# Cross-attention row maximum over partitions: GpSimd all-reduce in place of two groups of TensorE transposes, with exponentials two beats later

## The chip, the cores and the metric

One NeuronCore of a Trainium2 chip runs the whole program. The metric is the device time of one execution in microseconds (us). Engines: TensorE (PE in the profile, PEld for its weight loads), VectorE (DVE), ScalarE (ACT), GpSimd (POOL), and SyncE (SP), whose queue issues the DMAs.

## The reference

One layer of a perceiver on `x` (8 x 128 x 512, f32) with a context of 8 x 2048 x 512:

```python
x = x + xattn(layernorm(x), ctx, ctx)      # 16 heads of 32, 128 queries, 2048 keys
x = x + diff_attn(layernorm(x))            # two causal softmaxes a head, their difference
x = x + ffn(layernorm(x))                  # 8 experts with softmax gates
# within xattn:
scores = einsum('bhqd,bhkd->bhqk', q, k) / sqrt(32)
attn = softmax(scores, axis=-1)
ctx = einsum('bhqk,bhkd->bhqd', attn, v)
```

The change is in xattn alone, in the maximum that softmax subtracts.

## The kernel before

The program is a row of stages, each a block of its own on all engines: queries and weights, cross attention, output projection, the projections of self attention, differential attention, experts. Cross attention (`cross_attention`, L318 to L762) is the longest.

**Slots.** The work of cross attention is cut into 32 slots (8 batches times G = 4 groups of HG = 4 heads). A slot has four chunks of 512 keys. The order of work is written out by hand in beats, eight to a slot. `steps(beat, first, every, count)` says which item of a kind falls on a beat, and each engine runs the same loop over all beats, doing what the beat asks of it in the order of its own code.

**What a beat holds on PE** (L622 to L640). Every beat projects one unit of keys or values, twelve matmuls (L560, L567, through `product`, L43 to L45). Even beats also transpose context (L552), multiply one chunk of exponentials by the values (`outputs`, L601) and make one chunk of scores (`column_scores`, L587). Once a slot `denominators` (L611) multiplies the summed exponentials by ones. Beats that come up below, modulo 8: score chunks 0 to 3 of a slot on beats 4, 6, 0 and 2 (20, 22, 24, 26 for slot 0). All score chunks share one set of PSUM banks, `psS`, so PE waits for `s_moved` before the next.

**The maximum.** Scores lie with keys over the partitions and (head, query) along the free dimension, so the maximum over keys is one over chunks and partitions. DVE folds each chunk into `mx` (L759 copies the first piece of a slot, L762 folds the other fifteen); there is one `mx`. Then PE transposes `mx` (`turn("M", ...)`, beat 27), DVE reduces it to `top` (L726), ACT spreads that (L700), PE transposes back (`turn("B", ...)`, beat 28) and ACT copies the result to `mb` (L692). So every partition has one maximum for a head and a block of 128 queries.

**After the maximum.** ACT moves each score chunk from PSUM to one of BUFS = 6 buffers `s` (L713, on the beat after its scores). DVE subtracts `mb` from it (L733), ACT takes the exponential (L705), PE reads it for the outputs (L601) and POOL adds it up in `acc`: one add for chunk 0 (L512), two for each other (L517). POOL's chunk 0 waits for the denominators of the slot before (`od_full`). ACT may fill a buffer again when PE and POOL are done with its old content (`pv_done`, `sum_done`, L709 to L712).

**Banks.** Context transposes, projections and both kinds of turn share three PSUM banks `work` in a ring (`RING`, L379 to L391).

**Elsewhere** POOL broadcasts a row over partitions once in each of three later stages (`partition_broadcast`, L827, L1168, L1504), each time followed by `tensor_tensor` operations (L831, L1184, L1508).

## Time and profile before

| what | value |
|---|---|
| time, median of 3 runs | 1859.81 us (1859.74 to 1862.59) |
| the profiled execution's own time | 1860.6 us |
| its span in the trace | 1858.2 us |
| mean granted TensorE clock over the span | 0.955 |
| PE busy, share of the span | 1716.2 us, 92% |
| DVE busy | 1224.5 us, 66% |
| ACT busy | 962.7 us, 52% |
| POOL busy | 776.3 us, 42% |

The profiled execution's time is its span and 2.4 us around it. Times in rows count from the start of the span. Busy shares are means over stages with different limits; a sum for a change in cross attention has to be read from that stage.

### The profile page before, as it was taken

Reading aid. Unit: us, or ns where it says so; the run is one execution under the profiler, and the core shown is the slowest. Engines: PE = TensorE matmul, PEld = TensorE weight load, DVE = VectorE, ACT = ScalarE, POOL = GpSimd, SP = SyncE. Lnnn points to the kernel's source line nnn. Section 1 sums busy time; section 2 is a strip of 40 time slices with the busy share of each in tenths; the row PEclk is TensorE's granted clock in tenths of the full one; section 3 lists DMA queues with packets and bytes.
Section 4 is the critical chain, followed back from the end, with each engine's and each line's share of the span. In section 5 each row is a group of like instructions: output and inputs, shape, how many; then the busy total and the mean of one; then the engine's idle time right before and its main releaser. Section 6 shows DMA issues by size and latency. Waiting matters only on the chain. (4 is left out here: it accounts for less than half of the span.)

```text
span 1858.2 us, 36962 instructions
## 1 busy us (share of the span) xinstructions
PE 1716.2 (92%) x15305; PEld 1377.4 (74%) x15320; DVE 1224.5 (66%) x1631; ACT 962.7 (52%) x1470; POOL 776.3 (42%) x343
## 2 busy tenths in 40 slices
PE   6899999999999999999999997538999689879999
PEld 5688888888888888888888875437887466658886
DVE  5126887887887787787787788957332677753223
ACT  2236666666666666666666665533220677731000
POOL 0002555555555555555555555662000466622210
PEclk9999999999999999999999998658999899989999
DMA  4211111111111111110110102103650533201101
GB/s 162 69 46 38 38 29 40 38 28 40 38 30 38 38 34 34 38 40 28 38 41 27 38 7 71 44 29 131 201 179 14 159 92 90 68 24 46 45 23 45
DMA packets 104189, 104.94 MB, mean 56 GB/s; under 512 B 7263, under 2 KB 72799, under 8 KB 104044
## 3 DMA queue, kind: packets, MB, share of 16 engines
q1 hardware_dynamic: 104044, 102.83, 18.2%
q8 instruction: 113, 1.85, 0.4%
q14 instruction: 32, 0.26, 0.0%
HBM read 79.74 MB, written 23.07 MB: 55 GB/s over the span
## 5 line engine op out<-in xcount | busy, mean ns | idle before, releaser
L517 POOL TENSOR_TENSOR b_acc<-b_acc,b_s 128x1024 f32<-128x1024 f32 x192 | 525.7, 2738 | 294.6 <-ACT b_s L705 282.3
L733 DVE TENSOR_TENSOR b_s<-b_s,b_mb 128x2048 f32<-128x2048 f32 x128 | 372.5, 2912 | 15.7 <-ACT b_mb L692 15.7
L762 DVE TENSOR_TENSOR b_mx<-b_psS,b_mx 128x512 f32<-128x512 f32 x480 | 331.1, 690 | 44.2 <-PE b_psS L587 31.1
L705 ACT ACTIVATE b_s<-b_s 128x2048 f32<-128x2048 f32 x128 | 245.1, 1915 | 89.3 <-DVE b_s L733 89.3
L713 ACT ACTIVATE b_s<-b_psS 128x2048 f32<-128x2048 f32 x128 | 241.1, 1884 | 50.8 <-DVE b_mx L762 50.4
L43 PE MATMUL b_work<-cT,wkT 128*128 128x512 f32 x512 | 211.0, 412 | 0.0
L43 PE MATMUL b_work<-wvT,cT 128*128 128x512 f32 x512 | 209.4, 409 | 0.0
L512 POOL TENSOR_TENSOR b_acc<-b_s 128x1024 f32<-128x1024 f32 x32 | 80.8, 2525 | 290.8 <-PE b_psO L611 179.8
L44 PE MATMUL b_work<-cT,wkT 128*128 128x512 f32 x512 | 201.0, 393 | 0.0
L45 PE MATMUL b_work<-cT,wkT 128*128 128x512 f32 x512 | 200.7, 392 | 0.0
L45 PE MATMUL b_work<-wvT,cT 128*128 128x512 f32 x512 | 200.2, 391 | 0.0
L44 PE MATMUL b_work<-wvT,cT 128*128 128x512 f32 x512 | 200.0, 391 | 0.0
L587 PE MATMUL b_psS<-b_q,b_kT 32*128 32x128 f32 x4096 | 157.4, 292 | 15.1 <-ACT b_s L713 15.1
L664 ACT ACTIVATE b_kT<-b_work,b_bk 128x512 f32<-128x512 f32 x128 | 88.1, 688 | 157.4 <-PE b_work L45 155.0
L587 PEld LDWEIGHTS b_psS<-b_q,b_kT 32*128 32x128 f32 x4096 | 132.3, 194 | 41.6 <-issue 41.4
L601 PE MATMUL b_psO<-b_s,v_sb 128*32 128x128 f32 x4096 | 147.3, 289 | 15.6 <-ACT b_s L705 12.9
L601 PEld LDWEIGHTS b_psO<-b_s,v_sb 128*32 128x32 f32 x4096 | 111.9, 115 | 44.3 <-issue 43.7
L752 DVE TENSOR_TENSOR cT<-b_work,cT 128x512 fp32r<-128x512 f32 x128 | 87.3, 683 | 84.4 <-ACT cT L697 84.4
L1648 DVE SCALAR_TENSOR_TENSOR x<-f_ps,f_gate,x 128x512 f32<-128x512 f32 x64 | 47.9, 750 | 119.8 <-PE f_ps L45 119.3
L43 PEld LDWEIGHTS b_work<-cT,wkT 128*128 128x128 f32 x512 | 96.6, 189 | 30.1 <-issue 5.6
L43 PEld LDWEIGHTS b_work<-wvT,cT 128*128 128x128 f32 x512 | 96.1, 188 | 24.4
L45 PEld LDWEIGHTS b_work<-cT,wkT 128*128 128x128 f32 x512 | 96.7, 189 | 21.5
(221 smaller groups left out, 3036.7 us busy)
## 6 DMA issues: line engine op xcount, KB each, us to landing
cin<-in_ctx SPq DMA_DIRECT2D x64, 512.0 KB, 3.7
q_scratch<-d_st SPq DMA_DIRECT2D x32, 256.0 KB, 2.5
k_scratch<-d_st SPq DMA_DIRECT2D x32, 256.0 KB, 2.5
e_q<-q_scratch SPq DMA_DIRECT2D x16, 512.0 KB, 3.5
k_sb<-k_scratch SPq DMA_DIRECT2D x64, 128.0 KB, 3.6
experts_sb<-in_L_ffn_expert_w SPq DMA_DIRECT2D x8, 1024.0 KB, 5.2
x_sb<-in_x SPq DMA_DIRECT2D x2, 1024.0 KB, 7.1
q_scratch<-a_q SPq DMA_DIRECT2D x4, 512.0 KB, 3.2
```

The source lines that it names most:

```text
L43: nc.tensor.matmul(out, lhs[0], rhs[0], start=first, stop=False)
L44: nc.tensor.matmul(out, lhs[0], rhs[1], start=False, stop=False)
L45: return nc.tensor.matmul(out, lhs[1], rhs[0], start=False, stop=last)
L517: nc.gpsimd.tensor_tensor(acc[:, :, :], acc[:, :, :], s[:, buf, 2 * i:2 * i + 2, :], ALU.add).then_inc(sum_done, 1)
L587: last = nc.tensor.matmul(psS[:, j, t * P:(t + 1) * P], kT[h, at + t * P:at + (t + 1) * P], q[h, m % 3, :], start=True, stop=True)
L601: last = nc.tensor.matmul(psO[j * HD:(j + 1) * HD, 0:P], v[:, at + j * HD:at + (j + 1) * HD], s[:, n % BUFS, i, j * P:(j + 1) * P], start= ...
L664: nc.scalar.activation(kT[:, at:at + 512], work[i % BANKS][:, :], ACT.Identity, bias=bk[:, u:u + 1]).then_inc(k_done, 1)
L705: nc.scalar.activation(part, part, ACT.Exp, scale=SCALE).then_inc(exp_done, 1)
L713: nc.scalar.activation(s[:, n % BUFS, :, :].rearrange("p t (j q) -> p t j q", j=HG), psS[:, :, :].rearrange("p j (t q) -> p t j q", t=CHUN ...
L733: nc.vector.tensor_tensor(s[:, n % BUFS, :, :], s[:, n % BUFS, :, :], mb[:, :].rearrange("p (o n) -> p o n", o=1).broadcast_to([P, CHUNK, ...
L752: nc.vector.tensor_tensor(context_place(cT[1], p, n), two(work[RING["T", p, n] % BANKS]), f32(context_place(cT[0], p, n)), ALU.subtract).t ...
L762: nc.vector.tensor_tensor(mx[:, :, :], part, mx[:, :, :], ALU.max).then_inc(mx_done, 1)
```

## The change

The new kernel has POOL reduce `mx` over the partitions with one `partition_all_reduce` for each slot, [128 x 512] to [128 x 512], straight to `mb`. Both turns on PE, the reduction on DVE and two ACT copies for each slot are removed, and their bank uses with them. `mb` has two buffers in place of one. The maximum stands in POOL's order on beat 27, behind the sums of beat 26 and ahead of those of beat 28. Subtractions, exponentials, outputs, sums and denominators come two beats later, and `s` has seven buffers. DVE's first piece of a slot's `mx` (L759) now waits for `mb_done`, the end of the all-reduce of the slot before.

```diff
--- before.py
+++ after.py
@@ -328,8 +328,8 @@
         SLOTS = B * G
         SLOT = 8
         CHUNK = 4
-        BUFS = 6
-        FIRST, LAST = -SLOT, (SLOTS + 4) * SLOT + 3
+        BUFS = 7
+        FIRST, LAST = -SLOT, (SLOTS + 4) * SLOT + 5
         ADDS = 2 * CHUNK - 1
         MAXIMA = CHUNK * CHUNK
 
@@ -353,27 +353,21 @@
         def move_step(beat):
             return score_step(beat - 1)
 
-        def turned_slot(beat):
-            return steps(beat, 27, SLOT, SLOTS)
-
-        def spread_slot(beat):
-            return steps(beat, 28, SLOT, SLOTS)
-
         def exp_step(beat):
-            return steps(beat, 30, 2, SLOTS * CHUNK)
+            return steps(beat, 32, 2, SLOTS * CHUNK)
 
         def value_step(beat):
 
-            early, late = steps(beat, 32, 2, SLOTS * CHUNK), steps(beat, 33, 2, SLOTS * CHUNK)
+            early, late = steps(beat, 34, 2, SLOTS * CHUNK), steps(beat, 35, 2, SLOTS * CHUNK)
             if early is not None and early % CHUNK:
                 return early
             return late if late is not None and late % CHUNK == 0 else None
 
         def sum_slot(beat):
-            return steps(beat, 40, SLOT, SLOTS)
+            return steps(beat, 42, SLOT, SLOTS)
 
         def normal_slot(beat):
-            return steps(beat, 40, SLOT, SLOTS)
+            return steps(beat, 42, SLOT, SLOTS)
 
 
         BANKS = 3
@@ -384,10 +378,6 @@
             if (x0 := projected(beat)) is not None:
                 p0, u0 = x0
                 RING["KV"[u0 // CHUNK], p0, u0 % CHUNK] = len(RING)
-            if (s0 := turned_slot(beat)) is not None:
-                RING["M", s0, 0] = len(RING)
-            if (s0 := spread_slot(beat)) is not None:
-                RING["B", s0, 0] = len(RING)
         UNITS = list(RING)
 
         def key_place(b, g, c):
@@ -409,9 +399,7 @@
         q = sb("b_q", [P, 3, P])
         s = sb("b_s", [P, BUFS, CHUNK, HG * P])
         mx = sb("b_mx", [P, HG, P])
-        top = sb("b_top", [P, 2, HG])
-        spread = sb("b_spread", [P, HG, P])
-        mb = sb("b_mb", [P, HG * P])
+        mb = sb("b_mb", [P, 2, HG * P])
         acc = sb("b_acc", [P, 2, HG * P])
         rD = sb("b_rD", [P, P])
         oq = sb("b_oq", [P, P])
@@ -430,8 +418,6 @@
         v_done = sem("b_v_done")
         mx_done = sem("b_mx_done")
         s_moved = sem("b_s_moved")
-        top_done = sem("b_top_done")
-        spread_done = sem("b_spread_done")
         mb_done = sem("b_mb_done")
         s_full = sem("b_s_full")
         sub_done = sem("b_sub_done")
@@ -501,7 +487,8 @@
         @block.gpsimd
         def _(pool):
             nc.gpsimd.memset(ones[:, :], 1.0).then_inc(const, 1)
-            for n in range(SLOTS * CHUNK):
+
+            def sums(n):
                 m, c = divmod(n, CHUNK)
                 buf = n % BUFS
                 pool.wait_ge(exp_done, n + 1)
@@ -517,6 +504,21 @@
                         nc.gpsimd.tensor_tensor(acc[:, :, :], acc[:, :, :], s[:, buf, 2 * i:2 * i + 2, :],
                                                 ALU.add).then_inc(sum_done, 1)
 
+            def maximum(m):
+
+                pool.wait_ge(mx_done, (m + 1) * MAXIMA)
+
+                reached(pool, sub_done, (m - 1) * CHUNK)
+                nc.gpsimd.partition_all_reduce(mb[:, m % 2, :], mx[:, :, :].rearrange("p j q -> p (j q)"),
+                                               P, RMAX).then_inc(mb_done, 1)
+
+            for beat in range(FIRST, LAST):
+                if (n := exp_step(beat)) is not None:
+                    sums(n)
+                n = score_step(beat - 1)
+                if n is not None and n % CHUNK == CHUNK - 1:
+                    maximum(n // CHUNK)
+
         def sums_of(n):
 
             m, c = divmod(n, CHUNK)
@@ -534,12 +536,8 @@
                         pe.wait_ge(split_done, m * CHUNK + n + 1)
                     elif kind == "K":
                         pe.wait_ge(k_done, m * CHUNK + n + 1)
-                    elif kind == "V":
+                    else:
                         pe.wait_ge(v_done, m * CHUNK + n + 1)
-                    elif kind == "M":
-                        pe.wait_ge(top_done, m + 1)
-                    else:
-                        pe.wait_ge(mb_done, m + 1)
                 return work[i % BANKS]
 
             def transposes(p, n):
@@ -612,13 +610,6 @@
                                                 acc[:, i, j * P:(j + 1) * P], start=i == 0, stop=i == 1)
                 last.then_inc(od_full, 1)
 
-            def turn(kind, m, src, ready, count):
-                bank = bank_of((kind, m, 0))
-                pe.wait_ge(ready, count)
-                for j in range(HG):
-                    last = nc.tensor.transpose(bank[:, j * P:(j + 1) * P], src[:, j, :], ident[:, :])
-                last.then_inc(work_full, 1)
-
             for beat in range(FIRST, LAST):
                 if (x0 := transposed(beat)) is not None:
                     transposes(*x0)
@@ -634,10 +625,6 @@
                         keys(p, u)
                     else:
                         values(p, u - CHUNK)
-                if (m := turned_slot(beat)) is not None:
-                    turn("M", m, mx, mx_done, (m + 1) * MAXIMA)
-                if (m := spread_slot(beat)) is not None:
-                    turn("B", m, spread, spread_done, m + 1)
 
         def context_place(a, p, n):
 
@@ -684,21 +671,11 @@
                                 out = rows[:, :, at[0]:at[0] + P]
                             nc.scalar.activation(out, work[i % BANKS][:, :].rearrange("p (g r) -> p g r", g=G),
                                                  ACT.Copy).then_inc(v_done, 1)
-                if (m := spread_slot(beat - 1)) is not None:
-                    i = RING["B", m, 0]
-                    act.wait_ge(work_full, i + 1)
-
-                    reached(act, sub_done, m * CHUNK)
-                    nc.scalar.activation(mb[:, :], work[i % BANKS][:, :], ACT.Copy).then_inc(mb_done, 1)
                 if (x0 := transposed(beat)) is not None:
                     p, n = x0
                     i = RING["T", p, n]
                     act.wait_ge(work_full, i + 1)
                     nc.scalar.activation(context_place(cT[0], p, n), two(work[i % BANKS]), ACT.Copy).then_inc(hi_done, 1)
-                if (m := spread_slot(beat)) is not None:
-                    act.wait_ge(top_done, m + 1)
-                    nc.scalar.activation(spread[:, :, :], top[:, m % 2, :].rearrange("p (j o) -> p j o", o=1)
-                                         .broadcast_to([P, HG, P]), ACT.Copy).then_inc(spread_done, 1)
                 if (n := exp_step(beat)) is not None:
                     act.wait_ge(sub_done, n + 1)
                     part = s[:, n % BUFS, :, :].rearrange("p t n -> p (t n)")
@@ -718,13 +695,6 @@
         def _(dve):
             dve.wait_ge(bias_in, 32)
             for beat in range(FIRST, LAST):
-                if (m := spread_slot(beat)) is not None:
-                    i = RING["M", m, 0]
-                    dve.wait_ge(work_full, i + 1)
-
-                    reached(dve, spread_done, m - 1)
-                    nc.vector.tensor_reduce(top[:, m % 2, :], work[i % BANKS][:, :].rearrange("p (j k) -> p j k", j=HG),
-                                            AX.X, ALU.max).then_inc(top_done, 1)
                 if (n := exp_step(beat)) is not None:
                     m, c = divmod(n, CHUNK)
                     dve.wait_ge(s_moved, n + 1)
@@ -732,7 +702,7 @@
                         dve.wait_ge(mb_done, m + 1)
                     nc.vector.tensor_tensor(
                         s[:, n % BUFS, :, :], s[:, n % BUFS, :, :],
-                        mb[:, :].rearrange("p (o n) -> p o n", o=1).broadcast_to([P, CHUNK, HG * P]),
+                        mb[:, m % 2, :].rearrange("p (o n) -> p o n", o=1).broadcast_to([P, CHUNK, HG * P]),
                         ALU.subtract).then_inc(sub_done, 1)
                 if (m := normal_slot(beat)) is not None:
                     g = m % G
@@ -756,6 +726,9 @@
                     for t in range(CHUNK):
                         part = psS[:, :, t * P:(t + 1) * P]
                         if n % CHUNK == 0 and t == 0:
+                            if n:
+
+                                dve.wait_ge(mb_done, n // CHUNK)
                             nc.vector.tensor_copy(mx[:, :, :], part).then_inc(mx_done, 1)
                         else:
                             dve.wait_ge(mx_done, n * CHUNK + t)
```

## Rows read from the trace of the kernel before

**Rows 1.** Windows of the cross attention: busy time and instructions of each engine, clock, DMA.
```profile
200.00:1130.00 930.00, 930.00 (x10559) 751.97 (x10558) 737.99 (x751) 613.08 (x589) 505.81 (x189) 1.00 0.12 34
1130.00:1248.00 118.00, 58.36 (x950) 46.23 (x948) 94.35 (x74) 53.62 (x34) 80.06 (x28) 0.60 0.15 47
```

**Rows 2.** Timeline, PE, one slot: start, duration, instructions merged.
```profile
608.83 1.17 PE L587 MATMUL b_psS<-b_q,b_kT 32*128 32x128 f32 x32
...
616.04 0.64 PE L611 MATMUL b_psO<-b_acc,b_ones 128*32 128x128 f32 x16
616.62 1.17 PE L587 MATMUL b_psS<-b_q,b_kT 32*128 32x128 f32 x32
...
625.06 1.08 PE L601 MATMUL b_psO<-b_s,v_sb 128*32 128x128 f32 x32
626.07 1.17 PE L587 MATMUL b_psS<-b_q,b_kT 32*128 32x128 f32 x32
...
632.76 0.60 PE L619 MATMUL b_work<-ident,b_mx 128*128 128x128 f32 x4
633.20 0.60 PE L552 MATMUL b_work<-ident,cin 128*128 128x128 f32 x4
```

**Rows 3.** Timeline, DVE: the first piece of a slot's maximum.
```profile
153.26 0.68 DVE L759 COPY b_mx<-b_psS 128x512 f32<-128x512 f32 x1
...
1119.76 0.69 DVE L759 COPY b_mx<-b_psS 128x512 f32<-128x512 f32 x1
...
1182.40 0.68 DVE L759 COPY b_mx<-b_psS 128x512 f32<-128x512 f32 x1
```

**Rows 4.** Timeline, POOL, around partition_broadcasts: idle time before in brackets.
```profile
1253.80 1.04 POOL L827 PARTITION_BROADCAST c_bo<-c_bo_row  x1 [9.23 <-issue]
1264.12 10.04 POOL L831 TENSOR_TENSOR x<-x,c_bo 128x512 f32<-128x512 f32 x8 [9.27 <-issue]
...
1452.86 0.31 POOL L1168 PARTITION_BROADCAST e_coef<-e_coef_row  x1 [6.65 <-issue]
1463.02 2.03 POOL L1184 TENSOR_TENSOR e_sm<-e_sm,e_cf 128x512 f32<-128x512 f32 x2 [9.84 <-issue]
...
1662.99 4.57 POOL L1508 TENSOR_TENSOR f_ws<-experts_sb,f_ws 128x2048 fp32r<-128x2048 f32 x1 [6.92 <-issue]
```

**Rows 5.** Groups of instructions, POOL: count, busy, mean ns of one, idle before.
```profile
L1184 POOL TENSOR_TENSOR e_sm<-e_sm,e_cf 128x512 f32<-128x512 f32 x64 | 73.5, 1150 | 61.2 <-DVE e_cf L1378 50.7 <-issue 9.8
L1190 POOL TENSOR_TENSOR e_root<-e_ms,e_expo 128x16 f32<-128x16 f32 x8 | 23.3, 2907 | 7.1 <-DVE e_ms L1406 7.0
```

**Rows 6.** Timeline, DVE and PE, where PE waits for the move of scores.
```profile
1136.13 2.85 DVE L762 TENSOR_TENSOR b_mx<-b_psS,b_mx 128x512 f32<-128x512 f32 x4
...
1141.04 2.09 PE L587 MATMUL b_psS<-b_q,b_kT 32*128 32x128 f32 x32 [4.05 <-ACT b_s L713]
...
1171.33 1.76 PE L587 MATMUL b_psS<-b_q,b_kT 32*128 32x128 f32 x32 [2.23 <-ACT b_s L713]
```

**Rows 7.** Timeline, POOL, chunks 0 and 1 of a slot's sums.
```profile
616.87 2.39 POOL L512 TENSOR_TENSOR b_acc<-b_s 128x1024 f32<-128x1024 f32 x1 [6.34 <-PE b_psO L611]
619.40 4.88 POOL L517 TENSOR_TENSOR b_acc<-b_acc,b_s 128x1024 f32<-128x1024 f32 x2
```

**Rows 8.** Instructions of L733, DVE, and of L517, POOL: least, median and longest ns.
```profile
L733 DVE TENSOR_TENSOR b_s<-b_s,b_mb x128: 2277/2794/4448, 157.3 to 1228.1; 128x2048 f32<-128x2048 f32 x128
...
L517 POOL TENSOR_TENSOR b_acc<-b_acc,b_s x192: 2337/2407/4353, 170.2 to 1242.2; 128x1024 f32<-128x1024 f32 x192
```

**Rows 9.** Timeline, PE, a stretch behind idle time early in cross attention.
```profile
60.14 1.09 PE L552 MATMUL b_work<-ident,cin 128*128 128x128 f32 x4 [2.37 <-DMA cin<-in_ctx]
...
65.72 0.45 PE L45 MATMUL b_work<-cT,wkT 128*128 128x512 f32 x1
```

**Rows 10.** Timeline, DVE: last piece of slot 0's maximum; and PE: the last denominators.
```profile
145.74 2.86 DVE L762 TENSOR_TENSOR b_mx<-b_psS,b_mx 128x512 f32<-128x512 f32 x4
...
1244.62 1.08 PE L611 MATMUL b_psO<-b_acc,b_ones 128*32 128x128 f32 x16 [8.04 <-POOL b_acc L517]
```

## The prediction

> **What bounds the kernel now.** I began with the windows of the cross attention. From 200 to 1130 us PE is busy all 930 us at a granted clock of 1.00 (the 2.4 GHz level), DVE for 738, ACT for 613, POOL for 506 [rows 1]: this stretch is as long as PE's list. Behind it the projections have run out, and a slot is paced by the chain between PE, DVE and ACT: PE is busy 58 of 118 us, the clock falls to 0.60 [rows 1]. The first piece of a slot's maximum shows the rhythm: 28 slots from 153.26 to 1119.76, 34.52 us each, then two more in 62.64 us, and after the last of them 63.3 us until the last denominators end at 1245.70 [rows 3, 10]. The stages behind are not touched.
>
> Next I read POOL's timeline wherever it does what it does nowhere in cross attention, that is, around partition_broadcast. Each such instruction, and the first tensor_tensor behind it, stands behind idle time that no wait explains ("issue"): 9.23 and 6.65 us ahead of the broadcasts, 9.27, 9.84 and 6.92 ahead of the tensor_tensors [rows 4]. POOL changes kind of code there. In the new kernel it would do so twice in every slot.
>
> **What it removes.** The turn of `mx` puts the next unit of PE from 632.76 to 633.20: 0.44 us; the turn of `spread` has the same four transposes, so 0.88 us a slot, and PE's list becomes 33.64 us. The reduction on DVE and the two copies on ACT lay on engines with time to spare and count nothing. The ring of banks loses two uses, which can only help.
>
> **What it adds.** One all-reduce for each slot. The trace has none, so I bound its duration R. Below: no less than the broadcast of a 512-column row, 1.04 us [rows 4]. Above, if it went column by column like the power operation (2907 ns for 16 columns [rows 5]), 512 columns would take 93 us. In between: 128 partitions are seven halvings, and one two-input operation on 512 columns costs 1.15 us [rows 5], so 8.05 us. I take 8.05, because the halvings are what a maximum needs at least when it is done on whole vectors. Two passes for each halving would make 16.1.
>
> **The changes of code.** All-reduce and tensor_tensor alternate in POOL's order: chunk 0 and 1 of the sums, all-reduce, chunk 2 and 3. I assume that the all-reduce belongs with the broadcast. Ahead of it I take 6.65 us (the smaller, since the other may hold a DMA's landing), behind it the mean of the three, 8.68 [rows 4]. Of the same load the Trainium skill (GPSIMD Engine Reference, 2.1 Instruction dispatch) says that the first call to freshly loaded code pays about 6 us, 5.95 measured, with no instruction to be seen. The trace agrees for the way in (6.65); with 5.95 the sum below would be some 22 us less.
>
> **The new wait.** DVE's first piece of slot m+1 waits until the all-reduce of slot m ends, since there is one `mx`. Behind that wait stand, in DVE's own order, the rest of the chunk's maxima; ACT waits for those to move the scores, and PE for the move before its next score group. So a loop goes around once a slot:
> - From the end of the all-reduce through four maxima and a move to PE's scores of chunk 1: 1136.13 to 1141.04, 4.91 us [rows 6].
> - From there to the scores of chunk 3 PE must do its list: 608.83 to 626.07, 17.24, less one group of outputs (625.06 to 626.07, 1.01) that now falls outside: 16.23 [rows 2]. The two turns lie outside this part, so their removal doesn't shorten the loop.
> - The denominators come directly ahead of that group, and POOL's chunk 0 starts 0.25 us behind the group's start (616.62, 616.87) [rows 2, 7]. Chunks 0 and 1 take until 624.28, 7.41 us [rows 7]. L733 takes 2277 ns at least and 4448 at most, L517 2337 and 4353 [rows 8]: they exclude each other. One subtraction falls into these adds now that no reduction holds DVE up: 2.17. Together 9.83. The last chunk's maxima are done earlier than that (1.17 and 2.86 us) and hold nothing up.
> - Change of code 6.65, all-reduce 8.05.
>
> That is 21.14 + 9.83 + 14.70 = 45.67 us. PE has 33.64 to do and stands idle 12 us in one piece, ahead of chunk 1's scores. Behind 4.05 us of idle time that group took 2.09 us in place of 1.17 [rows 2, 6], the level of 1.2 GHz; and after such an interruption PE worked slowly from 60.14 to 65.72, which costs half of 5.58: 2.79 [rows 9]. So 48.46 us a slot.
>
> The other change of code, 8.68 us, comes behind the all-reduce, beside PE's list: chunks 2 and 3 (2 x 4.88) are then done 18.4 us after it, the denominators at about 21. With seven buffers ACT's move of chunk 1 needs chunk 2's sum, 13.6 us after the all-reduce against some 9 that it would like; PE would feel 2 to 4 us of this, but it runs beside the slow stretch just counted, so I add nothing. The later beats cost nothing in themselves: every item shifts alike. SP's queue holds the same loads and stores, those of `o` two beats later.
>
> **The sum.**
> - Slot 0: its maxima end at 148.60 [rows 10], the code is already loaded, so the next first piece comes at 156.65, not 153.26: +3.4.
> - 28 slots x 48.46 = 1356.9 against 966.5 [rows 3]: +390.4.
> - Two slots of the tail: scores follow each other every 7.57 us (1141.04 to 1171.33 is four [rows 6]), so 4.91 + 15.15 + 9.83 + 14.70 = 44.59 each, against 62.64 for both: +26.5.
> - The end: 44.59 for the last maximum, 8.68 to change code, chunks 2 and 3 at 9.76, denominators 1.33, four chunks 17.17, denominators 1.08: 82.6 against 63.3: +19.3.
>
> Together +439.6 us on the profiled execution's 1860.6: 2300 us. The median of the three runs is 0.8 us lower, which is nothing here. Every microsecond of R counts 32 times: 2300 + 32 x (R - 8.05).
>
> **Rivals.**
> 1. Column by column. For it speaks the power operation, 182 ns a column; against it, that a plain operation takes 2.2. With 93 us the time would be about 5020. The Trainium skill (GPSIMD Engine Reference, 3.2 Cross-partition) gives 247,699 ns for a reduction along the partition axis of 128 x 2048, a quarter of which, 62 us, is an estimate for 512 columns and would make 4026. No row here shows it. Chance 0.12.
> 2. No change of code between all-reduce and adds, with R near the broadcast's: the faster side. The loop is then 30.97 + R; it meets PE's list of 33.64 at R = 2.7 and the old slot of 34.52 at R = 3.55, and that is the point that decides. At R = 1.04: 28 x 0.88 = 24.6 us in the slots, 0.8 in the tail and 3.0 at the end, 1832 us. Against it stand the five gaps of rows 4. Chance 0.05. The same without a change of code but with R = 8.05: 39.0 and 2.8 for the clock, in all about 2085; chance 0.04, inside the range.
> 3. The move does not hide the latency but no engine waits long: if POOL fetches the other code while still adding, the gaps vanish under work. The gap behind L827 lies between two POOL instructions with nothing to cover it, so the trace can't exclude this; here the adds run to the last moment as well. It gives the times of rival 2, and its chance is counted there.
>
> **The numbers.** Forecast (code changed twice a slot, R between 1.04 and 16.1): chance 0.79. Low end: R = 1.04 gives 2076, and without the loss of clock (28 x 2.79) 1998. High end: R = 16.1 gives 2558, and if all four subtractions of a slot stand in POOL's way, 3 x 2.17 x 28 = 182 more, 2740. Range 2000 to 2740. A measurement can tell about 0.2%, 3.7 us, from no change. Faster 0.04, same 0.01, slower 0.95.
>
> **What would show it.** In the new profile: two gaps "issue" a slot in POOL's timeline, of 6 to 10 us; the all-reduce at about 8 us; the copy into `mx` idle before it with POOL as the releaser, some 16 us long; PE's L587 waiting for ACT's move about 12 us once a slot, its digits of clock below 9; first pieces 48 us apart. I am wrong if the gaps are absent, if R lies far from 8, or if the first piece does not wait for POOL.

## The result, and the profile after

The new kernel takes 2024.17 us, the median of four runs (2016.55 to 2042.29), beside 1860.92 for the kernel before (1859.74 to 1862.59): a ratio of 1.0891, 95% interval 1.0813 to 1.0968. It is slower by 163 us, where 440 was forecast. The profiled execution took 2019.06 us, its span 2017.3, which is 159.1 more than before. The new kernel's runs differ by 26 us, the old one's by 3; a possible reason is given behind the experiments.

The page of the new kernel, span, engines and the clock in 40 slices:

```profile
span 2017.3 us, 36462 instructions
...
PE 1740.0 (86%) x15064; PEld 1391.7 (69%) x15064; DVE 1201.1 (60%) x1599; ACT 925.2 (46%) x1406; POOL 829.0 (41%) x375
...
PEclk9999999999999989999998999655899989999999
```

No engine became the bound: every share has fallen. PE's own work grew by 24 us although 256 transposes are gone, because part of it ran at a lower clock. The digits hardly show that; a window over the slots does, and the tail behind them (columns: stretch, its length, PE, PEld, DVE, ACT, POOL busy with instructions, clock, DMA share, GB/s):

```profile
200.00:1290.00 1090.00, 979.61 (x10614) 786.15 (x10613) 748.71 (x742) 595.62 (x544) 570.92 (x223) 0.94 0.11 32
1290.00:1400.00 110.00, 40.48 (x688) 32.93 (x688) 67.39 (x54) 39.84 (x21) 66.97 (x25) 0.53 0.08 21
```

Before, PE was busy for all of such a stretch at clock 1.00 [rows 1]. Now it stands for 110 of 1090 us.

**Where the time came from.** Below, "the change in" is the idle time of POOL ahead of an all-reduce that follows adds, "the change back" the one ahead of the adds that follow an all-reduce. DVE's first pieces of a slot's maximum, now L732, and the last denominators on PE, now L609 (timelines: start, duration, idle time before and its releaser):

```profile
153.37 0.68 DVE L732 COPY b_mx<-b_psS 128x512 f32<-128x512 f32 x1
...
1254.31 0.69 DVE L732 COPY b_mx<-b_psS 128x512 f32<-128x512 f32 x1 [5.81 <-POOL b_mb L512]
...
1330.88 0.69 DVE L732 COPY b_mx<-b_psS 128x512 f32<-128x512 f32 x1 [5.67 <-POOL b_mb L512]
```

```profile
1407.39 1.08 PE L609 MATMUL b_psO<-b_acc,b_ones 128*32 128x128 f32 x16 [8.04 <-POOL b_acc L504]
```

Against [rows 3, 10]:

| part | before | after | added | forecast |
|---|---|---|---|---|
| until the first piece of slot 1 | 153.26 | 153.37 | +0.1 | +3.4 |
| 28 slots | 966.5 (34.52 each) | 1100.94 (39.32 each) | +134.4 | +390.4 |
| two slots of the tail | 62.64 | 76.57 | +13.9 | +26.5 |
| from there to the end of the last denominators | 63.3 | 77.6 | +14.3 | +19.3 |

Together +162.8; the stages behind gave back 3.7. So 28 slots hold nearly all of it, and there the forecast was 9.1 us a slot too high.

**One slot.** POOL's timeline from the end of one all-reduce (625.68 + 1.80 = 627.48) to the end of the next:

```profile
625.68 1.80 POOL L512 PARTITION_ALL_REDUCE b_mb<-b_mx  x1 [5.87 <-issue]
634.19 11.71 POOL L504 TENSOR_TENSOR b_acc<-b_acc,b_s 128x1024 f32<-128x1024 f32 x4 [6.71 <-issue]
...
650.25 2.39 POOL L499 TENSOR_TENSOR b_acc<-b_s 128x1024 f32<-128x1024 f32 x1 [4.36 <-PE b_psO L609]
652.79 4.88 POOL L504 TENSOR_TENSOR b_acc<-b_acc,b_s 128x1024 f32<-128x1024 f32 x2
663.56 1.80 POOL L512 PARTITION_ALL_REDUCE b_mb<-b_mx  x1 [5.89 <-issue]
```

DVE's, ACT's and PE's timelines in that slot:

```profile
627.58 0.69 DVE L732 COPY b_mx<-b_psS 128x512 f32<-128x512 f32 x1 [5.02 <-POOL b_mb L512]
...
656.02 3.80 DVE L703 TENSOR_TENSOR b_s<-b_s,b_mb 128x2048 f32<-128x2048 f32 x1
```

```profile
639.15 1.89 ACT L690 ACTIVATE b_s<-b_psS 128x2048 f32<-128x2048 f32 x1 [0.40 <-POOL b_acc L504]
```

```profile
632.50 2.09 PE L585 MATMUL b_psS<-b_q,b_kT 32*128 32x128 f32 x32 [2.62 <-ACT b_s L690]
...
642.22 1.17 PE L585 MATMUL b_psS<-b_q,b_kT 32*128 32x128 f32 x32
...
650.01 1.17 PE L585 MATMUL b_psS<-b_q,b_kT 32*128 32x128 f32 x32
```

The loop of the prediction is there step by step. The all-reduce ends, DVE starts its piece 0.10 us later, PE its scores of chunk 1 after 5.02 us (632.50), behind 2.62 us of idle time and at the lower of the clock's two levels, 1.2 GHz (2.09 us, where the same group takes 1.17 at 2.4 GHz). Chunk 3's scores follow 17.51 us on, chunk 0's sum 0.24 later, the adds of chunks 0 and 1 take 7.42, the change of code 5.89 and the all-reduce 1.80: 37.9 us. The mean spacing of all-reduces from slot 2 to slot 28 (slots counted from 0) is 39.4.

**Where other slots spend more.** Every one of these 26 slots has the same 5.0 us from the all-reduce to chunk 1's scores and nearly the same 15.4 us (13.5 to 13.8, and the 1.8 of the all-reduce) from chunk 3's scores to the end of the next all-reduce. What differs lies between. A row of the waits, 300 to 1200 us (total, times, longest), and one of the longer slots in ACT's and PE's timelines, behind an all-reduce that ended at 704.67:

```profile
ACT b_s L690 <- POOL b_acc L504: 42.1, 17, 4.6
```

```profile
718.71 1.88 ACT L690 ACTIVATE b_s<-b_psS 128x2048 f32<-128x2048 f32 x1 [2.66 <-POOL b_acc L504]
```

```profile
709.70 1.17 PE L585 MATMUL b_psS<-b_q,b_kT 32*128 32x128 f32 x32 [2.62 <-ACT b_s L690]
...
720.73 1.17 PE L585 MATMUL b_psS<-b_q,b_kT 32*128 32x128 f32 x32 [1.14 <-ACT b_s L690]
```

Here the scores of chunk 1 (709.70) stand behind the same 2.62 us of idle time and yet run at the upper level, and ACT's move of chunk 1 waits 2.66 us for chunk 2's sum, the last user of the buffer it wants. That sum stands behind the change back. This is a second loop, through the change back and the buffers of `s`. In 14 of the 26 slots the move waits for it by 2.0 to 4.8 us, and in 11 of those chunk 1's scores ran in 1.17 us. In the other 12 it waits less than 1 us, and in 11 of those chunk 1's scores took 1.5 to 2.1 us. So either the lower clock or the wait for the sum holds up a slot: chunk 2's scores come 10.6 us behind chunk 1's on average in the one kind of slot and 11.1 in the other.

The queue of POOL's instructions (POOLq) shows more of the idle time called "issue". All instructions of L512 and of L504 (counts; for L512 least, median and longest ns):

```profile
L512 POOLq MODIFY_POOL_CONFIG  x64: 1/13/30, 53.5 to 1359.6; - x64
L512 POOL PARTITION_ALL_REDUCE b_mb<-b_mx x32: 1802/1803/1807, 149.1 to 1366.4; - x32
  issue: 184.9, 31
...
L504 POOLq MODIFY_POOL_CONFIG  x62: 98/98/98, 191.6 to 1368.2; - x62
```

POOL's configuration is changed ahead of each all-reduce and again ahead of the adds behind it; 184.9 us in 31 gaps are 5.96 each on the way in. What POOL does in the gap is not seen: the two DMA queues of the kind "instruction" carried no more than before (111 and 33 packets against 113 and 32).

### The profile page after: what moved, and what is told of

Read it like the earlier page. It is cut to its first block and busy times, and to the rows that moved or that the text cites. A ratio compares the mean times of both kernels' runs of the same rounds, so it can differ in the third digit from the quotient of the medians.

```text
span 2017.3 us, 36462 instructions
## 1 busy us (share of the span) xinstructions
PE 1740.0 (86%) x15064; PEld 1391.7 (69%) x15064; DVE 1201.1 (60%) x1599; ACT 925.2 (46%) x1406; POOL 829.0 (41%) x375
## 5 line engine op out<-in xcount | busy, mean ns | idle before, releaser
L504 POOL TENSOR_TENSOR b_acc<-b_acc,b_s 128x1024 f32<-128x1024 f32 x192 | 522.7, 2722 | 246.0 <-issue 191.0
L585 PE MATMUL b_psS<-b_q,b_kT 32*128 32x128 f32 x4096 | 169.7, 308 | 143.0 <-ACT b_s L690 143.0
L585 PEld LDWEIGHTS b_psS<-b_q,b_kT 32*128 32x128 f32 x4096 | 144.3, 208 | 171.8 <-issue 166.6
L43 PE MATMUL b_work<-wvT,cT 128*128 128x512 f32 x512 | 222.6, 435 | 0.0
L43 PE MATMUL b_work<-cT,wkT 128*128 128x512 f32 x512 | 213.5, 417 | 0.0
L44 PE MATMUL b_work<-wvT,cT 128*128 128x512 f32 x512 | 212.0, 414 | 0.0
L45 PE MATMUL b_work<-wvT,cT 128*128 128x512 f32 x512 | 211.0, 412 | 0.0
L44 PE MATMUL b_work<-cT,wkT 128*128 128x512 f32 x512 | 203.7, 398 | 0.0
L45 PE MATMUL b_work<-cT,wkT 128*128 128x512 f32 x512 | 202.9, 396 | 0.0
L512 POOL PARTITION_ALL_REDUCE b_mb<-b_mx x32 | 57.7, 1803 | 280.6 <-issue 184.9
L43 PEld LDWEIGHTS b_work<-wvT,cT 128*128 128x128 f32 x512 | 104.9, 205 | 29.6 <-issue 3.4
L45 PEld LDWEIGHTS b_work<-wvT,cT 128*128 128x128 f32 x512 | 103.9, 203 | 24.4
L43 PEld LDWEIGHTS b_work<-cT,wkT 128*128 128x128 f32 x512 | 98.3, 192 | 30.9 <-ACT b_kT L651 5.6
```

The lines of the kernel that those rows point to most:

```text
L43: nc.tensor.matmul(out, lhs[0], rhs[0], start=first, stop=False)
L44: nc.tensor.matmul(out, lhs[0], rhs[1], start=False, stop=False)
L45: return nc.tensor.matmul(out, lhs[1], rhs[0], start=False, stop=last)
L504: nc.gpsimd.tensor_tensor(acc[:, :, :], acc[:, :, :], s[:, buf, 2 * i:2 * i + 2, :], ALU.add).then_inc(sum_done, 1)
L585: last = nc.tensor.matmul(psS[:, j, t * P:(t + 1) * P], kT[h, at + t * P:at + (t + 1) * P], q[h, m % 3, :], start=True, stop=True)
```

## The experiments

"Slot" is the mean spacing of all-reduces (or of what stands in their place) from slot 2 to slot 28; in the new kernel 39.4 us. The kernel before took 1859 to 1861.5 us beside each.

**1. No change of code.** The all-reduce is replaced by POOL's own kind of operation, `mx - mx`. No maximum is taken.

```diff
-                nc.gpsimd.partition_all_reduce(mb[:, m % 2, :], mx[:, :, :].rearrange("p j q -> p (j q)"),
-                                               P, RMAX).then_inc(mb_done, 1)
+                nc.gpsimd.tensor_tensor(mb[:, m % 2, :], mx[:, :, :].rearrange("p j q -> p (j q)"),
+                                        mx[:, :, :].rearrange("p j q -> p (j q)"), ALU.subtract).then_inc(mb_done, 1)
```

> The changed kernel with a tensor_tensor of POOL (mx minus mx, 512 columns) in the all-reduce's place: the exponentials are then taken without a maximum, and POOL never changes its code inside cross attention; every wait stays. Theory: the 5.9 us ahead of the all-reduce and the 6.7 to 7.1 us behind it are what lengthens the slot; without them DVE's wait for mb ends before it is reached and a slot falls from 39.4 us to PE's own 33.6, about 1835 us in all. Rival: the waits and the later beats cost the time whatever POOL runs there: the time stays above 1950.

1837.43 us (1836.13 to 1839.16), ratio 0.9883 [0.9864, 0.9902]. Its POOL timeline, and PE's scores of chunks 1 and 3:

```profile
617.72 3.08 POOL L512 TENSOR_TENSOR b_mb<-b_mx 128x512 f32<-128x512 f32 x1
621.92 6.80 POOL L504 TENSOR_TENSOR b_acc<-b_acc,b_s 128x1024 f32<-128x1024 f32 x2 [1.13 <-ACT b_s L682]
...
644.06 2.40 POOL L499 TENSOR_TENSOR b_acc<-b_s 128x1024 f32<-128x1024 f32 x1 [7.76 <-PE b_psO L609]
```

```profile
627.77 1.17 PE L585 MATMUL b_psS<-b_q,b_kT 32*128 32x128 f32 x32
...
643.82 1.17 PE L585 MATMUL b_psS<-b_q,b_kT 32*128 32x128 f32 x32
```

Here an instruction in that place took even longer than the all-reduce (3.08 us against 1.80), and yet the slot is 33.7 us, PE's list without the turns (33.64), and POOL has 7.76 us to spare. Chunk 3's scores come 16.05 us behind chunk 1's, which is PE's bare list for that part. Order, beats, buffers and waits are those of the new kernel. So the loss is not in them, but in what the all-reduce brings besides its length.

**2. The all-reduce twice**, the second waiting for the first.

```diff
+                nc.gpsimd.partition_all_reduce(mb[:, m % 2, :], row, P, RMAX).then_inc(first_done, 1)
+                pool.wait_ge(first_done, m + 1)
                 nc.gpsimd.partition_all_reduce(mb[:, m % 2, :], row, P, RMAX).then_inc(mb_done, 1)
```

> The changed kernel with the all-reduce done twice in a row, same source and result. Theory: the instruction takes the 1.80 us of its record and stands on the loop once a slot, so the second adds 32 x 1.8 = 58 us, about 2080. Rival: the record is too short and part of the gap ahead of it is the instruction's own work: then the second adds up to 5.9 + 1.8 us a slot, 246 us.

2091.32 us (2091.22 to 2101.61), 67 more than with one. POOL's timeline:

```profile
610.35 1.80 POOL L514 PARTITION_ALL_REDUCE b_mb<-b_mx  x1 [5.81 <-issue]
612.25 1.78 POOL L516 PARTITION_ALL_REDUCE b_mb<-b_mx  x1
```

The second stands 1.90 us behind the first's start, with no gap of its own; 32 x 1.9 is 61. The reduction costs what its record says, and the gap belongs to the change, not to the instruction.

**3. The change of code alone, in the kernel before.** Its turns stay; POOL broadcasts 32 columns once a slot to a tile that nobody reads, behind chunk 2's sum. The edit without the lines that make the tile and its semaphore:

```diff
+                if c == 2:
+                    reached(pool, spare_done, m)
+                    nc.gpsimd.partition_broadcast(spare[:, :], ones[0:1, :], P).then_inc(spare_done, 1)
```

> The kernel before, with a partition_broadcast of 32 columns into a spare tile behind each slot's chunk 2 on POOL; nobody waits for it. Theory: the two code changes around it (5.9 and 6.9 us) delay chunk 3's sum by 13.1 us, of which POOL's idle 5.0 hides a part; the denominators, 7.4 us away before, then wait 0.8 to 3 us a slot: 1885 to 1960 us. Rival: the instruction costs its record, 0.3 us, beside idle time: 1860.

2068.3 us (2061.05 to 2070.64), ratio 1.1112: 209 us for 32 instructions of 0.31 us. Both theories expected too little. POOL's timeline, PE's, and a row of the waits from 300 to 1200 us:

```profile
596.31 0.31 POOL L523 PARTITION_BROADCAST b_spare<-b_ones  x1 [5.87 <-issue]
603.80 6.74 POOL L519 TENSOR_TENSOR b_acc<-b_acc,b_s 128x1024 f32<-128x1024 f32 x2 [7.18 <-issue]
```

```profile
610.60 0.65 PE L616 MATMUL b_psO<-b_acc,b_ones 128*32 128x128 f32 x16 [2.13 <-POOL b_acc L519]
```

```profile
ACT b_s L718 <- POOL b_acc L519: 104.1, 22, 5.2
```

The two changes are 13 us in which POOL does nothing. With six buffers and the old beats, the late sum of chunk 3 holds up PE's denominators (2.13 us) and the buffer that ACT's move wants (4.7 us a time); that second wait was missing from my expectation. It also shows that the cost needs no all-reduce, and no wait of DVE.

**4. The reduction away, the changes of code kept.** A broadcast of `mx`'s first row stands in the all-reduce's place; no maximum over the partitions.

```diff
-                nc.gpsimd.partition_all_reduce(mb[:, m % 2, :], mx[:, :, :].rearrange("p j q -> p (j q)"),
-                                               P, RMAX).then_inc(mb_done, 1)
+                nc.gpsimd.partition_broadcast(mb[:, m % 2, :], mx[0:1, :, :].rearrange("p j q -> p (j q)"),
+                                              P).then_inc(mb_done, 1)
```

> The changed kernel with a partition_broadcast of mx's first row in the all-reduce's place (each exponent is then taken against the maximum over the keys of partition 0 only); code changes and waits stay. Theory: only the difference of the instructions goes, 1.80 - 1.04 us, 32 times: 24 us, about 2000. Rival: the reduction itself is the cost; the time falls to 1837, as with the tensor_tensor.

2016.73 us (2001.77 to 2023.98), which is 7 less than the new kernel and within its spread; the sum of 1.00 us in 32 slots, 32 us, did not come in full. In the profiled execution ACT's move of chunk 1 waited for chunk 2's sum in every slot, 4.1 us on average, so the second loop took back part of what the first had saved. The rival, that reducing is what costs, falls.

```profile
615.76 0.81 POOL L512 PARTITION_BROADCAST b_mb<-b_mx  x1 [6.01 <-issue]
```

**5. Two tiles `mx`**, so that DVE's first piece waits for the all-reduce of two slots before (`oq` shares its tile with `rD` to make room). The core of the edit:

```diff
-                            if n:
-                                dve.wait_ge(mb_done, n // CHUNK)
+                            reached(dve, mb_done, n // CHUNK - 1)
```

> The changed kernel with two mx buffers (and oq written over rD to make room), so that DVE no longer waits for the all-reduce before the next slot's first piece. Rival: that wait is the only one; a slot falls to PE's 33.6 us and the time to about 1840. Theory: a second loop is nearly as long. ACT may move chunk 1 only when chunk 2 of the slot before last is summed, and that sum stands behind both changes of code: 7.7 + 5.9 + 1.8 + 6.9 + 4.9 us after the scores of chunk 3, then the move 1.9 and PE's list from chunk 2 to chunk 3, 7.8: 36.9 us a slot with the clock up, against 37.9 for the first loop. So the time falls only to 1940 to 1990.

2086.03 us (2081.73 to 2092.46): slower than the new kernel by 62, where theory and rival both had it faster. POOL's and ACT's timelines and a row of the waits, 300 to 1200 us (total, times, longest; over the 21 times 7.5 a time):

```profile
605.48 3.75 POOL L512 PARTITION_ALL_REDUCE b_mb<-b_mx  x1 [6.02 <-DVE b_mx L733]
617.15 9.69 POOL L504 TENSOR_TENSOR b_acc<-b_acc,b_s 128x1024 f32<-128x1024 f32 x4 [7.92 <-issue]
```

```profile
622.02 1.88 ACT L690 ACTIVATE b_s<-b_psS 128x2048 f32<-128x2048 f32 x1 [7.74 <-POOL b_acc L504]
```

```profile
ACT b_s L690 <- POOL b_acc L504: 156.6, 21, 8.1
```

The wait of DVE is gone, and the loop now runs by another way: change in 6.0, all-reduce 3.77 (it shares its time with a subtraction of DVE), change back 7.92, chunk 2's sum 4.9, then ACT's move, which needs that sum for its buffer, some 2.1, PE's list to chunk 3's scores 9.65, and 0.25 + 7.42 for chunks 0 and 1: 42.0 us, measured 41.8. This is the wait of which the prediction said "I add nothing". It is a loop of its own, and here, with an all-reduce and a change back that are both longer than in the new kernel, it is longer than the first.

**6. The old beats** for subtractions, exponentials, outputs, sums and denominators, with seven buffers.

```diff
-            return steps(beat, 32, 2, SLOTS * CHUNK)
+            return steps(beat, 30, 2, SLOTS * CHUNK)
```

and all that follows it two beats earlier.

> The changed kernel with subtractions, exponentials, outputs, sums and denominators back on the beats of the kernel before; seven buffers kept. Theory: the loop through mb, the scores, chunk 3's maxima and POOL does not pass through them, except that one sum (chunk 2 in place of chunk 1) stands ahead of the all-reduce: 38.6 us a slot against 37.9 at like clock, so 2020 to 2050 us. Rival: the two beats' delay is what costs; the time falls below 1960.

2075.91 us (2072.8 to 2080.06). The two beats are worth 52 us to the new kernel. Its POOL and DVE timelines show the old cost that I had put into the forecast:

```profile
633.25 6.80 POOL L504 TENSOR_TENSOR b_acc<-b_acc,b_s 128x1024 f32<-128x1024 f32 x2 [4.17 <-ACT b_s L682]
```

```profile
606.83 0.69 DVE L732 COPY b_mx<-b_psS 128x512 f32<-128x512 f32 x1 [8.21 <-POOL b_mb L512]
```

Two adds take 6.80 instead of 4.88: one subtraction stands in their way, 1.9 us, and the exponential ahead of them has become part of the loop: 5.03 + 19.11 + 2.39 + 6.80 + 5.86 + 1.80 = 41.0, measured 41.4. The seventh buffer is part of the later beats. The new kernel with six buffers gives no time, since it comes to a deadlock: the move of the seventh chunk, on beat 33, needs the buffer that PE's outputs of beat 35 free, and these stand behind scores of beat 34 that wait for that move.

**7. The old beats and two tiles `mx`**: the edits of experiments 5 and 6 together, with one `mb` in place of the shared `oq` to make room. From the edit:

```diff
-        mx = sb("b_mx", [P, HG, P])
-        mb = sb("b_mb", [P, 2, HG * P])
+        mx = sb("b_mx", [P, 2, HG, P])
+        mb = sb("b_mb", [P, 1, HG * P])
```

> The all-reduce with the old beats, seven buffers, two mx and one mb. Neither DVE's wait for the all-reduce nor the wait for a buffer is then on a loop. Rival: POOL's own list is what is left, 19.0 us of sums, 1.8 and two code changes of 5.9 and 6.9, with a denominators' hand-over 34.5 us a slot, as before: 1860 to 1880 us. Theory: a third loop takes over. The denominators on the old beat wait for chunk 3's sum, which stands behind both code changes: 2.4 + 4.9 (6.8 with a subtraction in the way) + 5.9 + 1.8 + 6.9 + 4.9 after chunk 3's scores, then PE's list from the denominators to chunk 3's scores, 10.0: 39 to 41 us a slot, 2020 to 2080 us.

2061.36 us (2059.99 to 2062.62), slot 41.0. Even without DVE's wait and without the delay, a third way around closes: chunk 3's sum comes late behind the change back, the denominators wait for it (5.31 us), and POOL's next chunk 0 waits for the denominators. PE's timeline:

```profile
614.35 1.08 PE L609 MATMUL b_psO<-b_acc,b_ones 128*32 128x128 f32 x16 [5.31 <-POOL b_acc L504]
```

**8. The all-reduce ahead of chunk 1's sum** in POOL's order.

```diff
+                n = score_step(beat)
+                if n is not None and n % CHUNK == CHUNK - 1:
+                    maximum(n // CHUNK)
                 if (n := exp_step(beat)) is not None:
                     sums(n)
-                n = score_step(beat - 1)
-                if n is not None and n % CHUNK == CHUNK - 1:
-                    maximum(n // CHUNK)
```

> The changed kernel with the all-reduce ahead of chunk 1's sum in POOL's order, so that the change of code runs while DVE still folds the last chunk, and mb comes 4.9 us earlier. Rival: that takes 5 us out of the loop; a slot falls to 34 to 35 us and the time to about 1890. Theory: the sums of chunks 1, 2 and 3 now all stand behind both code changes; chunk 1's is done 22 us after the scores of chunk 3, the move of the next slot's chunk 0 waits for it, and the next scores of chunk 3 come no earlier than 39.8 us: the same time or up to 100 us more, 2024 to 2130.

2105.48 us (2101.72 to 2107.55), slot 42.6. The sum that left the first loop stands in the second one now: six adds in a row come behind the change back, and ACT's move of the next slot's chunk 0 waits for the first two of them, which are chunk 1's sum. POOL's timeline, and PE's:

```profile
614.45 16.59 POOL L504 TENSOR_TENSOR b_acc<-b_acc,b_s 128x1024 f32<-128x1024 f32 x6 [7.45 <-issue]
```

```profile
621.33 2.09 PE L585 MATMUL b_psS<-b_q,b_kT 32*128 32x128 f32 x32 [7.45 <-ACT b_s L690]
```

**9 and 10. What the clock costs.** Identity transposes that nobody reads fill PE's gap ahead of chunk 1's scores, 44 in the one kernel and 23 in the other.

```diff
+                    if n % CHUNK == 1 and n > CHUNK:
...
+                            for r in range(44):
+                                nc.tensor.transpose(bank[:, 0:P], ident[:, :], ident[:, :])
```

> The changed kernel with 44 transposes of the identity, 2.45 us, on PE ahead of chunk 1's scores, where it sits idle; they write to a bank that the next projection overwrites. Theory: the slow spell behind that idle time (the granted clock at its lower level) costs 1.3 to 4 us a slot; with the gap filled it goes, and a slot falls from 39.4 to about 37 us: 1940 to 1970 us in all. Rival: the slow spell runs beside POOL's and DVE's waits and costs nothing: 2024, or more by what the transposes overrun the gap.

With 44: 2003.27 us (2000.17 to 2006.44), 21 less than the new kernel, where 54 or more were expected. PE's timeline, and the window of the slots (columns as above):

```profile
627.06 5.02 PE L626 MATMUL b_work<-ident 128*128 128x128 f32 x44
632.01 1.17 PE L585 MATMUL b_psS<-b_q,b_kT 32*128 32x128 f32 x32
```

```profile
200.00:1290.00 1090.00, 1069.46 (x11916) 882.33 (x11914) 755.13 (x756) 606.03 (x550) 574.81 (x226) 0.99 0.10 32
```

The clock is 0.99 and chunk 1's scores take 1.17 us again, but 44 transposes took twice the time that I had assumed and ran about 2 us past the gap. The price had been on record: four transposes put the next unit off by 0.44 us [rows 2], 0.11 each. Over the slots, chunk 1's scores come 2.2 us later than in the new kernel, and chunk 3's follow them by the bare 16.0 us in place of 18.95; the difference is the 0.7 us by which the slot is shorter (38.7). With chunk 1's scores that late, ACT's move waits for chunk 2's sum by 0.2 us on average. So what went is the lower clock and the wait for the sum together. Then half as many transposes:

> As the run before with 23 transposes in place of 44. There the 44 took 4.95 us, not 2.45, and held the scores up: the move had let them go about 2.0 us earlier. 23 take 2.6 us, which is the gap. Theory: the clock stays up and nothing is held up: a slot goes from 38.6 to 36.6 us, against 39.4 of the changed kernel, so 1940 to 1950 us; what the lower clock takes is then some 2.7 us a slot. Rival: the clock's loss is only the 0.7 us a slot that the 44 transposes brought: 2003 or more.

With 23: 2047.24 us (2039.02 to 2052.99), slower than the new kernel, against the expectation. POOL's, DVE's, ACT's and PE's timelines:

```profile
635.82 2.73 PE L626 MATMUL b_work<-ident 128*128 128x128 f32 x23
...
649.35 1.80 PE L585 MATMUL b_psS<-b_q,b_kT 32*128 32x128 f32 x32 [2.58 <-ACT b_s L696]
```

```profile
640.42 11.74 POOL L504 TENSOR_TENSOR b_acc<-b_acc,b_s 128x1024 f32<-128x1024 f32 x4 [6.99 <-issue]
```

```profile
642.71 2.28 DVE L709 TENSOR_TENSOR b_s<-b_s,b_mb 128x2048 f32<-128x2048 f32 x1
```

```profile
647.33 1.88 ACT L696 ACTIVATE b_s<-b_psS 128x2048 f32<-128x2048 f32 x1 [4.10 <-POOL b_acc L504]
```

With the first gap filled, a subtraction of DVE comes between POOL's two adds of chunk 2, their sum is some 2 us later, and ACT's move waits 4.10 us for it. PE's gap has gone from chunk 1's scores to chunk 2's, and the clock falls there. The second loop sets the pace: 15.29 + 6.99 + 6.88 + 2.1 + 9.39 = 40.7, measured 40.4. In all 26 slots chunk 1's scores ran in 1.17 us, and in all of them the move waited for the sum, 4.1 us on average. With the clock up the other wait shows itself in every slot, so the lower clock taken away by itself gains nothing here. What it costs alone can't be read from these two kernels.

**11. The work of the turns done more cheaply.** In the kernel before, one matrix product of `mx` with a tile of 1/128 stands for both turns, DVE's reduction and ACT's spreading copy. The core of the edit; the second turn and the copies are taken out with it:

```diff
-                for j in range(HG):
-                    last = nc.tensor.transpose(bank[:, j * P:(j + 1) * P], src[:, j, :], ident[:, :])
+                last = nc.tensor.matmul(bank[:, :], share[:, :], src[:, :, :].rearrange("p j q -> p (j q)"),
+                                        start=True, stop=True)
```

It computes the same softmax, shifted by the mean of the 128 partitions' maxima instead of the largest. A shift leaves the quotients as they are, but the guard against overflow is weaker: a score may lie above the mean.

> The kernel before with, instead of both turns, the reduction on DVE and the spread on ACT, one fp32r matmul of mx by a 128 x 128 tile of 1/128: what softmax subtracts is then the mean of the 128 partitions' maxima, the same for all keys, so the softmax is the same in exact arithmetic, but the guard against overflow is weaker than with the maximum. Theory: PE's list is the bound, and a slot is 2 x 0.44 us shorter and one 512-column matmul, 0.23 us, longer: 28 x 0.65 = 18 us, and some 1 to 6 us in the tail: 1836 to 1842 us. Rival: the removed transposes fill gaps that stay; 1860.

1835.12 us (1833.58 to 1837.21), ratio 0.9866 [0.9849, 0.9882]: 1.3% less than the kernel before, clear of its noise, and less than the new kernel. PE's timeline and the window of the slots:

```profile
622.33 0.39 PE L614 MATMUL b_work<-b_mx,b_share 128*128 128x512 f32 x1
622.56 0.60 PE L548 MATMUL b_work<-ident,cin 128*128 128x128 f32 x4
```

```profile
200.00:1100.00 900.00, 900.00 (x10227) 725.14 (x10220) 726.13 (x717) 588.55 (x555) 549.33 (x188) 1.00 0.11 35
```

The product puts PE's next unit 0.23 us later, where each of two turns cost 0.44 [rows 2], and PE stays without a gap at clock 1.00.

## Why the prediction was wrong

Direction, place and mechanism held; the size did not. By its own steps:

1. **What is removed, 0.88 us a slot: right.** With no change of code the slot is 33.7 us, where 33.64 had been worked out, and the time 1837, where rival 2 had put 1832 (for R = 1.04; the instruction in that place took 3.08 here).
2. **R, 8.05 us: the step that failed.** "128 partitions are seven halvings, and one two-input operation on 512 columns costs 1.15 us", and "I take 8.05". The all-reduce takes 1.80 us, all 32 times (1802 to 1807 ns). It lies near the broadcast (1.04 us [rows 4]), which was the lower bound and stood in the nearest rows; I had priced it by an arithmetic operation instead. This is 6.25 us a slot, 200 of the 276 us between forecast and result. Rival 1 with its price of 5020 us, or 4026 by the estimate from the Trainium skill (GPSIMD Engine Reference, 3.2 Cross-partition), falls with it: for an all-reduce the measurement decides.
3. **One subtraction in the way of the adds, 2.17 us: not where it was put.** The adds of chunks 0 and 1 took 7.42 us undisturbed. The subtraction stood beside them and took 3.80 us, so DVE waited for POOL and not the other way. With the old beats the cost is there, 1.9 us (experiment 6): the delay by two beats removes it. The prediction had said that the later beats "cost nothing in themselves", but not that they gain. In the new kernel the subtraction falls into the adds of chunks 2 and 3 instead: four of them take 11.71 us, where two pairs of 4.88 would be 9.76.
4. **The change in, 6.65: 5.96 measured.** The Trainium skill (GPSIMD Engine Reference, 2.1 Instruction dispatch) has 5.95 for the first call to freshly loaded code; the trace agrees with it for the way in. Why the broadcast of [rows 4] stood 6.65 us behind is not shown. The change back was put at 8.68 and is 6.7 to 7.7. That POOL pays this again in every slot, in both directions, was the right step and is shown by experiments 1 to 4.
5. **5.02 us for DVE's part, against 4.91: right.** PE's list up to chunk 3's scores was put at 16.23 and is 16.05 where nothing disturbs it (experiment 1). In the new kernel it takes 17.51 in the slot shown and 18.95 on average.
6. **The clock, 2.79 us, and the buffer wait, nothing: together about right, in part by luck.** A slot is 48.46 - 39.37 = 9.09 us shorter than forecast, and the three terms above explain 6.25 + 2.17 + 0.69 = 9.11 of it. So what was put at 2.79 came out about the same: chunk 3's scores come 18.95 us behind chunk 1's, 2.9 more than the bare 16.05. But it is not the clock in every slot. In the 12 slots without the wait for chunk 2's sum these 2.9 us are 2.4, and the lower clock is what the rows show there; in the 14 slots with it they are 3.3, and the wait holds the slot. "It runs beside the slow stretch" was right in its result and not in its reason: in nearly every slot the two do not run beside each other, one comes in place of the other. The uneven slots (37.9 to 41.3 us) may also be what spreads the runs; that was not tested.
7. **The range, 2000 to 2740, held the time by luck.** R at the broadcast's price gives 2076 by the prediction's own sum, which is above the result. The low end reached below it only by leaving out the clock's loss, 28 x 2.79 = 78 us, and that loss, or the wait in its place, was there. What made up for it is that the sum had the subtraction and the change in too high, by 28 x (2.17 + 0.69) = 80 us. Rival 3, that the change of code hides under the adds, falls with the 31 gaps.

**Cause.** POOL changes its kind of code twice in each slot: 5.8 to 6.2 us in and 6.7 to 7.7 us back in the new kernel. Without it, 1837 us (experiment 1); with it and with almost nothing else, 2068 in the old kernel (experiment 3); with it and with the reduction gone, 2017 (experiment 4).

## What to carry to other kernels

Before an operation is moved to GpSimd, count how often that engine would change its kind of code in one turn of the loop: here a pair of changes cost 13 us of POOL, seven times the all-reduce itself. Where several loops of waits are about equally long, removing one wait or moving one step can gain nothing and lose 50 to 80 us (experiments 5, 6 and 8); write down every loop that goes through the disturbed engine, with its sum, before trusting the longest. And ask whether the result has to be so exact: a shift for a softmax can come from one matrix product of 0.23 us, as long as the weaker guard will do.

## What was not expected of the hardware

- A partition all-reduce of 128 x 512 float32 takes 1.80 us, about twice a broadcast of 512 columns (0.81 to 1.04).
- Beside a DVE subtraction with two SBUF operands it takes 3.75 us. POOL and DVE exclude each other here too, as adds and subtractions do [rows 8]. The Trainium skill (GPSIMD Engine Reference, 1. Specifications) has the two sharing SBUF interfaces, with contention when DVE has two SBUF inputs; the trace agrees.
- The change back (6.7 to 7.7 us in the new kernel) is longer than the change in (5.8 to 6.2).
- 44 transposes of the same tile in a row took 5.02 us, 0.11 each, and 23 took 2.73, 0.12 each, at clock 0.99 in the first case. I had assumed 0.056.
- A gap of 2.6 us on PE was followed by a group at the lower level in some slots (2.09 us at 632.50) and at the upper level in others (1.17 us at 709.70).
